# Four graph layers on one core: sums and spreads by rank, and the fourth layer's two edge passes in one

## The reference, cut to what matters

```python
# layer 0
agg = segment_sum(x[src], dst);  out = relu(agg @ W.T + b)
# layer 1
h = concat(x[src], x[dst], ea2) @ W1 + b1          # batchnorm over the edges, relu
out = segment_sum(h @ W2 + b2, src) / (counts + 1) + x
# layer 2, 8 heads
logits = sum(q[dst] * (k[src] + e)) / sqrt(16);  ex = exp(logits - segment_max(logits, dst)[dst])
conv = segment_sum(ex / denom[dst] * (v[src] + e), dst) + x @ Wskip + bskip
out = ln(gelu(h @ Wf1 + bf1) @ Wf2 + bf2 + h)      # h = ln(conv + x)
# layer 3, 4 heads
s = leaky_relu(src_score[src] + tgt_score[dst], 0.2);  s = exp(s - max(s))
out = segment_sum(proj[src] * s / (segment_sum(s, dst)[dst] + 1e-16), dst) + bias
```

## Time and profile before

| | |
|---|---|
| Median of 3 runs | 7105.09 us (7104.1 to 7108.03) |
| The profiled execution, own time | 7095.0 us |
| Its span, first to last instruction | 7093.3 us |
| Mean granted clock of TensorE | 0.829 |
| TensorE matmuls busy | 5014.6 us, 71% of the span |
| VectorE busy | 4761.2 us, 67% |
| GpSimd busy | 4617.0 us, 65% |
| ScalarE busy | 2418.4 us, 34% |
| DMA | 1118.61 MB, mean 158 GB/s |

### The profile page before, as it was taken

How to read it: one execution, slowest core, us unless ns; L and a number is a source line. 1 busy time by engine, 2 the same in 40 slices (tenths; PEclk the granted TensorE clock), 3 DMA queues, 4 the chain that set the end, 5 groups by cost and what they waited for, 6 DMA issues and landing times. The chain is left out here.

```text
span 7093.3 us, 130837 instructions
## 1 busy us (share of the span) xinstructions
PE 5014.6 (71%) x26221; PEld 3720.7 (52%) x26221; DVE 4761.2 (67%) x15639; ACT 2418.4 (34%) x6817; POOL 4617.0 (65%) x4240
## 2 busy tenths in 40 slices
PE   6887997997565466667882587887777689988000
PEld 4665885555555422226772475444444489978000
DVE  5667995444555599986774566877777545567666
ACT  0113663111222244441110134766666611133333
POOL 5773777776888788886662003788888767600776
PEclk9998998998878788888896798988888855589555
DMA  4666996886555598886664344444444333344567
GB/s 151 208 205 197 272 264 192 261 260 164 71 70 71 95 276 263 263 239 189 203 206 91 98 148 122 104 99 101 100 104 99 90 94 99 97 140 160 145 153 146
DMA packets 1373314, 1118.61 MB, mean 158 GB/s; under 512 B 144636, under 2 KB 1169658, under 8 KB 1373020
## 3 DMA queue, kind: packets, MB, share of 16 engines
q1 hardware_dynamic: 1148316, 787.09, 37.7%
q0 software_dynamic: 175616, 238.28, 18.3%
q10 hardware_dynamic: 49200, 91.54, 3.9%
HBM read 590.08 MB, written 549.45 MB: 161 GB/s over the span
## 5 line engine op out<-in xcount | busy, mean ns | idle before, releaser
L445 POOL DMA_INDIRECT l_nodes_ag<-agg,l_nodes_at x784 | 787.5, 1005 | 1141.0 <-DVE l_nodes_at L439 590.3
L1484 POOL DMA_INDIRECT agg<-l_edges_b_rows,l_edges_b_at x392 | 610.5, 1558 | 130.1 <-issue 70.0
L2254 PE MATMUL l_nodes_f<-l_nodes_h_t_s,w_f 128*128 128x512 f32 x784 | 454.3, 711 | 209.2 <-ACT l_nodes_act_t L2197 209.0
L1654 PE MATMUL l_nodes_y<-w_qkvs,l_nodes_x_t 128*128 128x512 f32 x784 | 448.3, 725 | 190.6 <-DVE l_nodes_qkvs L1573 190.5
L514 POOL DMA_INDIRECT to_col<-l_nodes_col_s,l_nodes_rank_at x392 | 390.9, 997 | 226.0 <-ACT l_nodes_col_s L1174 121.1
L1734 POOL DMA_INDIRECT l_edges_a_kv<-kv_tab,l_edges_a_src_s x392 | 392.3, 1001 | 188.1 <-issue 107.5
L2160 POOL DMA_INDIRECT tgt_first<-l_nodes_ext,l_nodes_first_s x392 | 414.5, 1057 | 125.6 <-issue 113.8
L2370 POOL DMA_INDIRECT l_edges_a_proj<-proj_tab,l_edges_a_src_s x392 | 371.3, 947 | 174.6 <-issue 108.4
L227 ACT COPY l_edges_a_rows<-l_edges_a_sums 128x128 f32<-128x128 f32 (+1 forms) x784 | 160.1, 214 | 945.0 <-PE l_edges_a_sums L213 860.9
L1586 POOL DMA_INDIRECT q_first<-l_nodes_qkvs,l_nodes_first_s x392 | 403.2, 1029 | 108.8 <-issue 98.8
L1243 POOL DMA_INDIRECT l_edges_a_at_row<-to_row,l_edges_a_row_i x392 | 378.3, 965 | 131.0 <-issue 105.5
(11 more groups left out here) (324 smaller groups left out, 14737.2 us busy)
## 6 DMA issues: line engine op xcount, KB each, us to landing
agg<-zeros ACTq DMA_DIRECT2D x98, 516.0 KB
l_nodes_xg<-x SPq DMA_DIRECT2D x196, 256.0 KB
kv_tab<-l_nodes_qkvs SPq DMA_DIRECT2D x98, 512.0 KB
agg<-l_edges_b_rows SPq DMA_DIRECT2D x98, 272.0 KB, 2.1
proj_tab<-l_nodes_ext SPq DMA_DIRECT2D x98, 264.0 KB, 3.5
agg<-l_edges_b_rows SPq DMA_DIRECT2D x98, 264.0 KB, 2.1
l_nodes_ag<-agg SPq DMA_DIRECT2D x98, 258.0 KB
l_nodes_ag_odd<-agg SPq DMA_DIRECT2D x98, 258.0 KB
```

The costliest lines, as they stand in the source:

```text
L445: pool.indirect_dma_start(ag[k][:, j, :], None, table, bass.IndirectOffsetOnAxis(at[k][:, j:j + 1].bitcast(U32), 0),).then_inc(a_in[k][j], 16)
L1484: pool.indirect_dma_start(agg1[j // 2], bass.IndirectOffsetOnAxis(at[k][:, j:j + 1].bitcast(U32), 0), rows[k][:, j, :], None, compute_op=A ...
L1654: pe.matmul(y[j][:], x2_t[k][:, j, :], w_qkvs[:], start=True, stop=True).then_inc(y_done, 1)
L2254: pe.matmul(f[m % 2][:], w_f1[:, m * P:(m + 1) * P], h_t_s[k][:], start=True, stop=True).then_inc(f_done, 1)
```

## The change

1. **Key lines as digits.** `rank_rows` also writes each rank as two bf16 digits. `window_steps` loads the 2 KB line of a group, TensorE multiplies it with `radix` into one PSUM bank, ScalarE copies it to SBUF, and VectorE marks from there. For that bank, `nodes_0` has one `col_p` in place of two.

```diff
 def window_steps(...):
-                sp.dma_start(keys[k][:], lines[bass.ds(n, 1)].to_broadcast([P, GE])).then_inc(line_in[k], 16)
+                sp.dma_start(line[k][:], lines[bass.ds(n, 1)].squeeze(0)).then_inc(line_in[k], 16)
...
+            def spread_line(pe, i, k):
+                n = place(i, k)
+                pe.wait_ge(line_in[k], i * 16 + 16)
+                if follows(i, k, 1):
+                    pe.wait_ge(line_copied, n)
+                pe.matmul(keys_p[:], radix[:], line[k][:], start=True, stop=True).then_inc(line_spread, 1)
...
+                act.copy(keys[k % 2][:], keys_p[:]).then_inc(line_copied, 1)
 def nodes_0():
-                y, row_p, col_p = ([ps(f"{n}{m}", [P, G, D]) for m in range(2)] for n in ("y", "row_p", "col_p"))
+                y, row_p = ([ps(f"{n}{m}", [P, G, D]) for m in range(2)] for n in ("y", "row_p"))
+                col_p = ps("col_p", [P, G, D])
...
                                 pe.wait_ge(row_done, n - 1)
-                                pe.wait_ge(col_done, n - 1)
+                            if follows(i, k, 1):
+                                pe.wait_ge(col_done, n)
...
-                        rotation(pe, groups, (2, spread), (8, turn_x1), (3, project), (9, project_x1))
+                        rotation(pe, groups, (0, lambda i, k: spread_line(pe, i, k)), (2, spread), (8, turn_x1), (3, project), (9, project_x1))
...
-                        rotation(act, groups, (5, lambda i, k: root(act, i, k)), (2, copy_a), (8, copy_x1), (7, apply), (10, lambda i, k: stage_rank(act, i, k)), (10, col))
+                        rotation(act, groups, (0, lambda i, k: copy_line(act, i, k)), (5, lambda i, k: root(act, i, k)), (2, copy_a), (8, copy_x1), (7, apply), (10, lambda i, k: stage_rank(act, act.copy, i, k)), (10, col))
```

```diff
+                        def clear(i, k):
+                            if k == 0:
+                                zero_rows(sp, agg2, i, cleared)
...
-                        pipeline(sp, pairs, (0, load))
+                        pipeline(sp, pairs, (0, load), (0, clear))
+                        sp.wait_ge(cleared, 16 * (pairs + 1))
```

```diff
+                        rotation(dve, groups, (0, stage), (2, score), (1, lambda i, k: mark_line(dve, i, k, tgt_spread)), (2, raise_top),
+                                 (2, lambda i, k: mark(dve, i, k, (3, 2))), (2, lower), (2, lambda i, k: mark(dve, i, k, (1, 0))),
+                                 (2, weigh), (2, carry))
...
+                        def raise_top(i, k):
+                            dve.wait_ge(top_turned, n + 1)
+                            dve.tensor_reduce(line_top[k % 2][:], top_p[:], AX.X, ALU.max).then_inc(line_topped, 1)
+                            dve.wait_ge(line_topped, n + 1)
...
+                            dve.tensor_tensor(top[k % 2][:], line_top[k % 2][:], was[:], ALU.max).then_inc(topped, 1)
+                        def lower(i, k):
+                            dve.wait_ge(top_spread, n + 1)
...
+                            dve.tensor_scalar(low[k][:], low_p[:], -1.0, None, ALU.mult).then_inc(lowered, 1)
...
+                        rotation(pe, groups, (2, turn_top), (0, lambda i, k: spread_line(pe, i, k)), (1, spread_tgt), (2, spread_top),
+                                 (3, total_messages))
...
+                        rotation(act, groups, (0, lambda i, k: copy_line(act, i, k)), (2, rise), (2, ease_carry),
+                                 (3, lambda i, k: empty(act, i, k, low)))
```

```diff
-                        rotation(pool, groups, (0, lambda i, k: fetch(pool, i, k)))
...
+                            for t in (0, 1):
+                                last = pool.tensor_scalar(hot[k % 2][t][:], keys[k % 2][:, t * P:], own_rank[:, t:t + 1], None, ALU.is_equal)
...
+                        rotation(pool, groups, (1, mark_rest), (5, lambda i, k: root(pool, i, k)))
```

More of the change, by code:

```diff
@@ L14 @@
+import math
 from contextlib import ExitStack
@@ L627, in _, with rank_rows @@
                         dve.tensor_copy(earlier[:], before_i[:]).then_inc(placed, 1)
[L628 removed]
+                        dve.wait_ge(placed, 3)
                         dve.tensor_scalar(node_col[:], high[:], -tiles / 2, None, ALU.add).then_inc(placed, 1)
[L630 to L631 removed]
+                        dve.tensor_tensor(opens[:], own[:], earlier[:], ALU.not_equal).then_inc(placed, 1)
+                        dve.wait_ge(placed, 5)
                 free()
[L634 removed]
+        def rank_rows(name, mark, local, base_i, line, last_of=None, rows=None, present=None):
             with ExitStack() as ctx:
@@ L838, in empty @@
                     act.wait_ge(stored, (n - RING + 1) * 16)
-                act.copy(rows[k][:], sums[k % 2][0][:]).then_inc(evacuated, 1)
+                for m in range(G // each):
+                    last = act.copy(rows[k][:, m * each:(m + 1) * each, 0:width], sums[k % 2][m][:])
+                if beside is not None:
+                    last = act.copy(rows[k][:, :, width:width + 1], beside[k][:].unsqueeze(1).to_broadcast([P, G, 1]))
+                last.then_inc(evacuated, 1)
             def store(sp, i, k):
@@ L1633, in apply @@
                             apply_norm(act, i, k, x2s[k], u[k])
-                        rotation(act, groups, (7, copy), (6, apply), (2, scale), (7, stage))
+                        rotation(act, groups, (7, copy), (6, apply), (2, scale), (7, lambda i, k: stage_rank(act, act.copy, i, k)))
                     @block.tensor
@@ L1725, in _ @@
-                        pipeline(dve, pairs, (2, add_e), (0, stage), (1, lambda i, k: compare(dve, i, k)), (2, score), (2, flatten))
+                            m = pair(i, k)
+                            dve.wait_ge(scored, place(i, k) + 1)
+                            if reuses(i) or k > 1:
+                                dve.wait_ge(s_turn, m)
+                            dve.tensor_copy(flat[:], scores[:, bass.ds(m * wide, wide)]).then_inc(s_flat, 1)
+                        rotation(dve, groups, (0, stage), (1, lambda i, k: mark_line(dve, i, k, q_spread)), (2, add_e), (2, score),
+                                 (3, flatten))
@@ L1986, in _ @@
+                        rotation(dve, groups, (0, differ), (1, lambda i, k: mark(dve, i, k)), (1, lambda i, k: mark_carry(dve, i, k)),
+                                 (1, weigh))
                     @block.scalar
@@ new lines, in edges_3 @@
+                low = [sb(f"low{k}", [P, 1]) for k in range(RING)]
+                ease = [sb(f"ease{k}", [P, 1]) for k in range(RING)]
+                mark, mark_carry, total, empty, store, settle, summed, evacuated = compact_steps(space, agg3, D + H3, ease)
+                tgt, at_rank, load_window, spread_line, copy_line, mark_line, window_in, hot_made, _, _ = window_steps(
+                    space, tgt_tab, H3, edge_base, edge_line)
+                src_s = [sb(f"src_s{k}", [P, G], I32) for k in range(RING)]
@@ L2464, in apply @@
                             apply_norm(act, i, k, last_x[k], u[k])
-                        rotation(act, groups, (0, stage), (3, lambda i, k: root(act, i, k)), (5, apply))
+                        rotation(act, groups, (0, lambda i, k: copy_line(act, i, k, (pool_made,))), (2, floor), (7, apply))
                 free()
@@ L2473, in gnn @@
             gather_sum_edges(count)
-            locate_sums(count, has)
+            flag_nodes(count, has)
             with nc.sbuf_tensor("local_node", [P, tiles], F32) as local_node:
-                rank_rows("node_ranks", has, local_node, node_base, node_line, rows=rank_row)
+                rank_rows("node_ranks", has, local_node, node_base, node_line, rows=sum_row, present=rank_row)
         nodes_0()
@@ L2482, in gnn @@
         segment_max()
-        weigh_edges("l2_edges_b", agg2, H2, v_edge, C2 ** -0.5, None)
+        edges_2b()
         nodes_2()
-        edges_3a()
-        weigh_edges("l3_edges_b", agg3, H3, p_edge, 1.0, gmax)
+        edges_3()
         nodes_3()
```

822 lines of the change are left out of this document (373 added, 449 removed).

## The result

The changed kernel takes 7441.3 us, median of 4 runs (7436.3 to 7444.2), the kernel before 7106.6 (7104.1 to 7112.7): ratio 1.047, interval 1.045 to 1.049. The forecast was 6975, in a range up to 7150. The profiled execution's own time is 7440.8, its span 7439.0, the mean granted clock 0.851.

The account below looks back on a forecast made before the run. No single bound: GpSimd's indirect DMAs set a floor of 490 to 502 us for some stages, TensorE and its clock weigh on others. Terms sum to -129.5 from 7095.0: 6965.5, or 6975.6 on the median's footing; range 6830 to 7150.

Parts of the forecast that it names:

- nodes_0: Stage nodes_0: with one col_p the engines wait on each other, 791 us against 582.7, +208 (bounds +150, +260).
- its own signs: Whole kernel: prediction is wrong if nodes_0 isn't the one stage that gets longer, or edges_3 isn't what gives most.
- edges_3: Merged edges_3a and l3_edges_b: 6.9 us a group, mean clock about 0.89, 696 us against 886.3, -190.
- edges_2a: Stage edges_2a: one window spread replaces key transposes, compares and copies; GpSimd's gathers bound it, 518 against 579.9, -62.
- the ring: In nodes_0 turn_x1, ScalarE's tail, project_x1 and the next spread follow one another, 7.7 us a group instead of 5.37.
- Rival B: nodes_0 is not coupled and stays at 583 or falls to its floor; whole 6767 or 6717; chance 0.08.
- VectorE sets the stage: nodes_3: gathers leave, VectorE bounds it at 4.6 us a group, 465 us, -59 (-80 to 0).
- rival A: edges_3 falls to the lower clock: at 9 us a group +16, whole 7181; stuck at half 7446; chance 0.14.
- the room: Between l0_edges and nodes_0: locate_sums' chain goes, node_ranks gains six short operations, together -15.5 us (-18 to -10).
- rival D: The clears in edges_1b collide with the accumulating DMAs, +109 instead of +10, whole 7074; chance 0.08.
- Rival C: edges_3 holds full clock, -258 in place of -190, whole 6907; chance 0.2.
- edges_2b: Stage edges_2b: compact products and a carry replace other records, 3.55 to 3.7 us a group instead of 3.86, -18.

Follow-up runs that it names:

- The run with apply outside the ring: Changed kernel with ScalarE's order in nodes_0 made copy_x1, rank, col, apply: 7201.6 us.
- the order change that undoes the coupling: Changed kernel with ScalarE's rank and col copies in nodes_0 put ahead of copy_a, copy_x1 and apply: 7125.7 us, beside 7099.8 for the kernel before.
- both orders changed: Changed kernel with nodes_3's apply ahead of floor on ScalarE and power ahead of marks on GpSimd: nodes_3 480.6 us, 455.4 on another kind of chip.
- the run with the three orders: Changed kernel with col ahead of copies and apply in nodes_0, apply ahead of floor and power ahead of marks in nodes_3: 6912.4 us, ratio 0.972.

## Why the prediction was wrong

The kernel got 335 us slower where 130 us less were forecast. Slower had a chance of 0.17, and the time lies beyond the range's end of 7150. By its own signs the prediction is wrong as well: nodes_0 isn't the one stage that gets longer, since nodes_3 does too. edges_3 gives most, but by 74.1 against edges_2a's 69.6.

**nodes_0: mechanism right, the length of a turn too short.** The forecast named the wait, the place and the ring. It priced the turn at 7.7 us from records at full clock, and put the clock's fall only into the range, up to +260. Measured: 9.1 us a turn, +341. Its steps between turn_x1 and the col copy came out right (0.75, 0.6, 2.2), and the spread of the turn shown was 1.0 longer at the lower clock. An estimate from the stage's clock says the same: 0.86 over 9.1 us is 2.5 us at half speed, in which 1.3 us are lost, and 9.1 less 1.3 is 7.8. The run with apply outside the ring shows it from the other side: 1.65 us less of waiting gave 2.4 a group, and the clock went to 0.97. So this ring, which makes TensorE wait, also lengthened its own TensorE part. Rival B, no coupling, is refuted: the order change that undoes the coupling gives back 308 us.

**nodes_3: the step that failed was "VectorE sets the stage".** I summed each engine's work (4.6, 3.2) and did not look for a ring. There was one, of the same kind as in nodes_0: spread_sums, floor, apply, the division, by way of `if reuses(i): dve.wait_ge(normed, ...)`. That wait stood in the kernel before, where apply had no TensorE-dependent step ahead of it. The change put floor there. Measured 682 in place of 465, 6.8 us a group in place of 4.6. With both orders changed it is 455.4, and VectorE starts a group every 4.5 us (79 groups from 6499.3 to 6849.2, with 8 us of waits), which is what the sum had given. So the work of VectorE was priced right and its order not read. The clock adds to it here too: at 0.74 for the stage the spread of the turn shown took 3.89 us, while at full clock in the run with the three orders it took 2.54:

```profile
6705.40 2.54 PE L400 MATMUL l_nodes_sums<-l_nodes_ag,l_nodes_at_rank 128*128 128x133 f32 x20
```

GpSimd's marks, whose price was open between 0.49 and 1.285 us, took more than the upper bound (1.57 us for the wide one), and still weren't in the ring:

```profile
L2405 POOL TENSOR_SCALAR l_nodes_at_rank<-l_nodes_keys,own_rank 128x512 f32<-128x512 f32 x98 | 153.9, 1570 | 325.9 <-PE l_nodes_sums L400 289.6 <-ACT l_nodes_keys L380 36.3
L2405 POOL TENSOR_SCALAR l_nodes_at_rank<-l_nodes_keys,own_rank 128x384 f32<-128x384 f32 x98 | 122.0, 1244 | 0.0
```

The Trainium skill, GPSIMD Engine Reference, 4.1, has one-input operations at about VectorE's line rate. The trace disagrees: the mark of 512 columns took 1.57 us on GpSimd in nodes_3, against 0.49 for the same operation on VectorE in nodes_0 before:

```profile
L485 DVE TENSOR_SCALAR l_nodes_hot<-l_nodes_keys,own_rank 128x512 f32<-128x512 f32 x98 | 48.0, 490 | 22.1 <-DMA l_nodes_keys<-node_line 8.2 <-issue 8.1 <-PE l_nodes_spread_a L1085 5.6
```

**edges_3: bound right, clock wrong.** TensorE's turn is 6.59 where I had 6.2, and it is the bound. The clock was to be 0.89 by likeness to l0_edges and was 0.80. The likeness was false: l0_edges also has four bf16 products of 392 columns a group, which the forecast itself cites in the earlier trace rows for another purpose. edges_3 has twenty records of 4 columns there. With 6.59 at full clock and the forecast's 11.7 at half, a clock of 0.80 makes about 8.0 us a group and some 800 us, an estimate; so this miss is the clock, and the 0.4 a group by which the turn itself is longer. The term was -74. It came near rival A, whose threshold was 825.8 us and a clock of about 0.74; with nodes_0 and nodes_3 as forecast, 812.2 would have left a gain of 14 us. That four bf16 products a group are what kept l0_edges at 0.99 is not shown: four of them added to edges_3 raised the clock only from 0.79 to 0.83.

The rule of the Trainium skill, TensorE: Matmul & The Clock Gate, Part 1, that a busy PE opens the gate, would have given 2.4 GHz in edges_3. The rows disagree, if busy means that matmuls are running: 0.80 at 98% busy, 0.95 at the same 98% when only the number of moving columns had changed.

**The small ones.** edges_2a (-69.6 for -62) and the room (-13.8 for -15.5) held. The clears in edges_1b cost nothing (-0.7), so rival D is refuted. Rival C, full clock in edges_3, is refuted by its 0.80. edges_2b gained 1 instead of 18: it has TensorE busy 365 of 377, so the compact products, which I had priced at 3.55 to 3.7 us a group, cost what the old ones did (3.84); what each part costs was not tried apart. nodes_1's +13 is not explained by any run.

The three misses together, 133 + 116 + 217 = 466, are nearly all of the 475 between the forecast of the profiled execution, 6965.5, and its 7440.8.

## What to carry to other kernels

When a buffer goes from two to one or a step is put into an in-order loop, write down for every new or old wait which step of which engine releases it and what stands ahead of that step in the same iteration; if the chain comes back to its start with the groups one apart, its sum is the loop's length, whatever the engines' totals say. Both rings here were opened by moving steps in an engine's list. And where products move few columns, read the granted clock before pricing TensorE at full speed: in edges_3, repeating four columns sixteen times took 15% off the stage.
